# Two attention layers with film on one core: VectorE's block turns ahead of h, bulk transfers moved on SP's queue, film steps, layer change and end reordered

## The reference

```
xn = layernorm(x) * norm_scale + norm_bias
q, k, v = xn @ Wq + bq, xn @ Wk + bk, xn @ Wv + bv        # masked rows: k = -inf (or -1e6), v = 0
q = softmax(q over the head's columns);  k = softmax(k over the 128 rows)
y = q @ (k^T @ v)                                          # per head
scale, shift = split(silu(cond) @ film_W + film_b)         # one row per sequence
h = layernorm(y) * film_norm_scale + film_norm_bias
h = h * (1 + scale) + shift
x = x + silu(h) @ Wo + bo
```

## Time and profile before

| | us |
|---|---|
| runs | 969.55, 980.11, 980.13 (median 980.11) |
| profiled execution, own time | 981.22 |
| profiled execution, span | 979.4 |
| TensorE busy | 873.1 (89%) |
| VectorE, ScalarE, POOL busy | 674.4, 609.8, 555.9 |
| mean granted TensorE clock | 0.955 |
| DMA, mean over the span | 173 GB/s |

### The profile page before, as it was taken

The page is one execution under the profiler, slowest core; times in us unless marked ns, Lnnn a source line. Parts: engine busy times, 40 slices in busy tenths (PEclk is TensorE's granted clock), DMA queues, the critical chain, the costliest instruction groups (busy, mean ns, idle before and its releaser), DMA issues. The chain is left out here.

```text
span 979.4 us, 19873 instructions
## 1 busy us (share of the span) xinstructions
PE 873.1 (89%) x6581; PEld 733.7 (75%) x6581; DVE 674.4 (69%) x1349; ACT 609.8 (62%) x1445; POOL 555.9 (57%) x744
## 2 busy tenths in 40 slices
PE   5878898999889999999489899999899999999975
PEld 4657776888778887888367788887788787887753
DVE  6776675776777776777547777776777777775632
ACT  5354765665766667766455876677666776666442
POOL 2455655556556765666456665665567656665310
PEclk9898998999999999999789999999999999999987
DMA  8667666646465554554626555554565555553310
GB/s 302 217 202 223 199 197 218 211 144 200 157 205 161 162 170 141 163 166 149 209 81 221 169 174 160 182 173 170 155 192 200 182 184 176 174 188 134 123 64 32
DMA packets 115419, 169.80 MB, mean 173 GB/s; under 512 B 11742, under 2 KB 84566, under 8 KB 115318
## 3 DMA queue, kind: packets, MB, share of 16 engines
q1 hardware_dynamic: 114816, 168.08, 53.3%
q10 hardware_dynamic: 502, 0.46, 0.2%
HBM read 95.61 MB, written 72.88 MB: 172 GB/s over the span
## 5 line engine op out<-in xcount | busy, mean ns | idle before, releaser
L660 ACT ACTIVATE Z<-QT,FC,FA 128x128 f32<-128x128 f32 x240 | 99.1, 484 | 182.4 <-DMA QT<-qy_turned 182.4
L546 POOL TENSOR_TENSOR HL<-H,HH 128x512 fp32r<-128x512 f32 x60 | 77.4, 1291 | 200.4 <-ACT HH L693 191.5
L821 PE MATMUL PS<-XH,WH_k 128*128 128x256 f32 x512 | 151.3, 296 | 3.9 <-DVE WL_k L300 3.9
L821 PE MATMUL PS<-XL,WH_k 128*128 128x256 f32 x512 | 146.1, 285 | 0.0
L821 PE MATMUL PS<-XH,WL_k 128*128 128x256 f32 x512 | 146.0, 285 | 0.0
L821 PE MATMUL PS<-WH_o,HH 128*128 128x512 f32 x248 | 110.3, 445 | 13.1 <-issue 6.9
L821 PE MATMUL PS<-WH_v,XH 128*128 128x512 f32 x256 | 102.3, 400 | 14.9 <-POOL WL_v L300 12.0
L821 PE MATMUL PS<-WH_q,XH 128*128 128x512 f32 x256 | 103.4, 404 | 9.6 <-ACT Z L688 9.6
L626 ACT ACTIVATE SK<-SK,KN 128x128 f32<-128x128 f32 x256 | 98.9, 388 | 9.3 <-DVE KN L1112 9.3
L821 PE MATMUL PS<-WL_o,HH 128*128 128x512 f32 x248 | 103.2, 416 | 0.0
L821 PE MATMUL PS<-WH_o,HL 128*128 128x512 f32 x248 | 102.6, 414 | 0.0
(11 more groups left out here) (144 smaller groups left out, 2157.0 us busy)
## 6 DMA issues: line engine op xcount, KB each, us to landing
qy_turned<-QS SPq DMA_DIRECT2D x60, 512.0 KB, 3.0
QT<-qy_turned SPq DMA_DIRECT2D x240, 128.0 KB, 2.9
k_turned<-KT SPq DMA_DIRECT2D x32, 512.0 KB, 4.3
EK<-k_turned SPq DMA_DIRECT2D x128, 128.0 KB, 2.8
x_turned<-XS SPq DMA_DIRECT2D x30, 512.0 KB, 2.7
XT<-x_turned SPq DMA_DIRECT2D x120, 128.0 KB, 2.9
out_x<-X SPq DMA_DIRECT2D x32, 256.0 KB, 2.9
X<-in_x SPq DMA_DIRECT2D x9, 512.0 KB, 4.6
```

Of the source, the lines that this page charges most:

```text
L546: eng.tensor_tensor(hl_of(o), h_of(o), hh_of(o).bitcast(F32), ALU.subtract).then_inc(pool_hl, 1)
L660: z = eng.activation(Z[:, c * P:c * P + P].rearrange("p (q n) -> p q n", q=Q), src, ACT.Identity, bias=FC[l][:, c, b:b + 1], scale=FA[l][: ...
L821: mm = eng.matmul(dst, left[a](c), right[b](c), start=(c == 0 and a + b == 0), stop=(c == C - 1 and a == 1))
```

## The change

FILM_SLOTS becomes [2, 3, 7, 11, 15, 19]. On VectorE turn_x and turn_queries move in front of keys and h_mul, stat_x behind values. On SP the mask load moves from the front of an even step behind the reads; x loads and stores are done in even steps, two tiles at a time for the stores. On ScalarE h_high stands behind x_turned. Around step 32 the splits, loads and biases are reordered, and one more chunk of the value weights' low half is made on VectorE. At the end, the last tile's y gets a buffer (XN) and a PSUM bank of its own, and the order is written anew on four engines.

```diff
-        FILM_SLOTS = [1, 2, 6, 9, 12, 15]
+        FILM_SLOTS = [2, 3, 7, 11, 15, 19]
...
         def norm_at(s):
-            return stats_at(s)
+            return [4, 5, 6] if s == 1 else [s + 4] if 2 < s < NT - 4 else []
...
-        LOW_ON_DVE = [range(C), range(C), [1, 2, 3], range(2), [0, 2], [0, 2], [0, 2], [0, 2]]
+        LOW_ON_DVE = [range(C), range(C), [1, 2, 3], range(2), [0, 2], [0, 1, 2], [0, 2], [0, 2]]
...
+        def y_of(o):
+            return XN[:, 1, :] if o == t2 else YN[:, :]
+
+        def bank_ty(o):
+            return B_ATT if o == t2 else B_TY
...
 SP:
             for s in range(1, NT - 1):
                 if s == B:
                     load_second(eng, 6)
-                if s % 2 == 0 and s + 2 < NT:
-                    eng.wait_ge(dve_ka, s)
-                    load_mask(eng, s // 2 + 1)
                 if s > 1:
                     for g in x_pair_at(s):
                         write_x(g)
+                if s == B - 1:
+                    load_second_bias(2, pool_bo)
                 write_qy(s)
                 if s > 1:
                     for g in x_pair_at(s):
                         read_x(g)
+                if s == B - 1:
+                    load_second(eng, 5, [0])
                 read_qy(s)
                 if s == B - 1:
-                    load_second(eng, 5)
+                    load_second(eng, 5, [1, 2, 3])
+                    load_second_bias(0, dve_v)
                 if s % 2 == 1:
                     place_keys(s // 2)
...
+                if s % 2 == 0 and s + 2 < NT:
+                    eng.wait_ge(dve_ka, s)
+                    load_mask(eng, s // 2 + 1)
                 if s == B - 1:
-                    load_second_bias(0, dve_v)
-                    load_second_bias(2, pool_bo)
                     load_second_bias(1, dve_q)
-                if s == B + 1:
+                if s == B + 2:
                     load_second(eng, 7)
-                if s >= B + 5:
+                if s >= B + 6 and s % 2 == 0:
+                    store(s - B - 6)
                     store(s - B - 5)
-                if s == 3:
+                if s == 4:
                     eng.wait_ge(pe_film, 2)
                     wait_split(3)
-                if 3 <= s < 11:
-                    load_x(s + 3)
+                if 4 <= s < 20 and s % 2 == 0:
+                    load_x(4 + s // 2)
...
 POOL:
+                if s == B:
+                    split_low(eng, 5, low_on_pool(5))
                 if s >= 3:
                     root_y(s - 3)
-                if s == B:
-                    split_low(eng, 5, low_on_pool(5))
...
+                if s == B - 1:
+                    split_low(eng, 4, low_on_pool(4))
                 if s == B:
                     split_low(eng, 6, low_on_pool(6))
                 if 2 * FIRST <= s + 2 < NSTEP:
                     x_low(s + 2)
                 normalise_keys(s)
-                if s == B - 1:
-                    split_low(eng, 4, low_on_pool(4))
...
 ScalarE:
+                if s > 1:
+                    for n in norm_at(s):
+                        norm_x(n)
+                if s == B:
+                    split_high(5)
                 if 0 <= o:
                     film(o)
                 if s >= 3:
                     norm_y(s - 3)
-                if 0 <= o:
-                    h_high(o)
-                if s == B:
-                    split_high(6)
...
-                if s in FILM_SLOTS:
-                    conditioning_sums(FILM_SLOTS.index(s))
...
                 if s > 2 and m < NSTEP:
                     x_turned(m)
+                if 0 <= o:
+                    h_high(o)
+                if s in FILM_SLOTS:
+                    conditioning_sums(FILM_SLOTS.index(s))
+                if s == B - 1:
+                    split_high(4)
+                if s == B:
+                    split_high(6)
                 if s >= 2:
                     exp_k(i)
-                if s == B - 1:
-                    split_high(4)
...
-                if s == B - 1:
-                    split_high(5)
...
 TensorE:
-                if s == 1:
-                    conditioning(0)
...
+                if s == B:
+                    output(o)
+                    attention(j)
+                queries(i)
...
             values(t2)
+            attention(t0)
+            queries(t2)
+            turn_y(t9)
             turn_queries(t1)
-            queries(t2)
-            attention(t0)
-            turn_y(t9)
+            mix(t0)
             output(LAST_Y - 1)
-            mix(t0)
             attention(t1)
             turn_queries(t2)
+            mix(t1)
+            turn_y(t0)
+            attention(t2)
+            mix(t2)
             output(t9)
-            mix(t1)
-            attention(t2)
-            turn_y(t0)
-            mix(t2)
+            turn_y(t1)
             output(t0)
-            turn_y(t1)
+            turn_y(t2)
             output(t1)
-            turn_y(t2)
             output(t2)
...
 VectorE:
-                if s > 1:
-                    for n in stats_at(s):
-                        stat_x(n)
                 if s == B:
                     split_low(eng, 5, LOW_ON_DVE[5])
-                if s == 1:
-                    turn_queries(0)
+                if 1 < s < NT - 4:
+                    turn_x(s + 4)
                 if s > 0:
+                    turn_queries(s - 1)
                     keys(i)
                 if 0 <= o:
                     h_mul(o)
-                if 1 < s < NT - 4:
-                    turn_x(s + 4)
-                if s > 1:
-                    turn_queries(s - 1)
                 if s >= 3:
                     turn_y(s - 3)
...
                 if s > 0:
                     values(i)
-                key_sums(i)
+                if s > 1:
+                    for n in stats_at(s):
+                        stat_x(n)
                 if s == B - 1:
                     split_low(eng, 4, LOW_ON_DVE[4])
...
+                key_sums(i)
...
             mixed(t9)
+            turn_keys(t2)
             h_mul(LAST_Y - 1)
             values(t2)
             queries(t2)
+            mixed(t0)
             h_mul(t9)
             h_low(t9)
             add_x(LAST_Y - 1)
-            mixed(t0)
             mixed(t1)
-            add_x(t9)
+            mixed(t2)
             h_mul(t0)
             h_low(t0)
-            mixed(t2)
+            add_x(t9)
```

More of the change, by code:

```diff
@@ L301, in split_low, with load_second @@
                                   ALU.subtract).then_inc(low_w[w][c], 1)
-        def load_second(eng, w):
+        def load_second(eng, w, chunks=range(C)):
             src = weights[1][w % 4].rearrange("(c p) n -> p c n", p=P)
-            for c in range(C):
+            for c in chunks:
                 if w > 4:
@@ L631, in norm_y @@
                 eng.wait_ge(pool_y, o + 1)
-                eng.activation(YN[:, :], YN[:, :], ACT.Identity, bias=NBY[:, :], scale=RSY[:, :]).then_inc(act_yn, 1)
+                y = y_of(o)
+                eng.activation(y, y, ACT.Identity, bias=NBY[:, :], scale=RSY[:, :]).then_inc(act_yn, 1)
             def exp_q(j):
@@ L774, in _ @@
                     exp_k(n)
-                for n in norm_at(s):
-                    norm_x(n)
                 if s == 1:
+                    for n in norm_at(s):
+                        norm_x(n)
                     split_high(3)
-                if s == B - 1:
-                    split_high(5)
                 if s == B + 3:
@@ L783, in _ @@
             film(LAST_Y - 1)
+            h_high(LAST_Y - 1)
             norm_y(t9)
             exp_q(t0)
-            h_high(LAST_Y - 1)
+            heads(t0)
             values(t2)
-            heads(t0)
             film(t9)
             exp_q(t1)
-            heads(t1)
             h_high(t9)
             norm_y(t0)
+            heads(t1)
             exp_q(t2)
@@ L873, in turn_y @@
                 for c in range(C):
-                    mm = eng.transpose(bank(B_TY, c * P, P), YN[:, c * P:c * P + P], ident[:, :])
+                    mm = eng.transpose(bank(bank_ty(o), c * P, P), y_of(o)[:, c * P:c * P + P], ident[:, :])
                 mm.then_inc(pe_ty, 1)
@@ L1181, in mixed @@
                 eng.wait_ge(dve_yr, j + 1)
-                then(eng.bn_stats(BNY[:, :], YN[:, :]))
+                then(eng.bn_stats(BNY[:, :], y))
                 eng.wait_ge(pool_y, j)
@@ L1330, in _ @@
                     split_low(eng, 6, LOW_ON_DVE[6])
+                if s == B - 1:
+                    queries(i)
+                key_sums(i)
                 if s == 0 or s == B:
                     turn_keys(i)
-                queries(i)
-                if s != 0 and s != B:
+                for n in keys_at(s):
                     turn_keys(i)
+                    keys(n)
+                if s != B - 1:
+                    queries(i)
+                if 0 < s < NT - 2 and s != B:
+                    turn_keys(i)
```

(6 more changed lines are left out.)

25 lines of the change are left out of this document (13 added, 12 removed).

## The result

The changed kernel took **901.26 us** in the median (900.45 to 902.12), the kernel before 979.30 beside it (969.55 to 980.13): ratio 0.922 (0.917 to 0.928). The forecast was 911.

What follows compares the result with a forecast made beforehand. A circuit through three engines and SP's queue, not TensorE, was taken to pace plain steps. Terms -30, -8, -4, -11 and -16 summed to -69 on 981.2, giving 912, or 911 us against the median; range 893 to 948.

Steps and rivals of the forecast that it cites:

- Plain steps, -30: Steps 6 to 61 without film pieces or layer change: 43.4 us of excess, 30 gained by a shorter circuit, 13 left.
- sign "3.8": Plain steps: the write of q and y would come 3.8 us after film's start, against 4.93 before.
- film to film under 12.9: Plain steps: one film start to the next would take under 12.9 us, a sign of the forecast holding.
- waits on HL: TensorE waiting for h_low's result ahead of the output; appearing in plain steps, they would show the forecast wrong.
- Costed at nothing: Moving h_high on ScalarE would cost nothing; with its cover gone, 0.8 us per pair of steps, some 22 us.
- Film, -8: The four film steps in steps 6 to 31: excess falls from 20.4 us to 12, at 3.0 each.
- Rival (c): Odd film steps cost what step 9 cost, 8.4 us each: 21.6 us on the forecast, 933 us; chance 0.07.
- Start, -4: First steps: 4 us gained, with film piece 0 out of step 1 and turns some 3 us earlier; bounds -9, +3.
- Layer change, -11: Step 32: from 34.7 us to about 24, with the output's bias row loaded earlier; bounds -4, -15.
- End, -16: Behind step 61: 12 us of TensorE's idle time and 4 of the clock's part gained; bounds -8, -23.
- (a): Plain steps: the circuit stays, through exp_q and a QT landing lengthened by stores; 942 us, chance 0.20.
- (b): Every step's output: the wait moves from EK to HL, slower, +85 us over 50 steps; 1026 us, chance 0.04.

Runs made afterwards that it cites:

- e1: The changed kernel with turn_x and turn_queries put back behind h_mul on VectorE; 923.98 us.
- e2: The kernel before with only turn_x and turn_queries moved ahead of keys and h_mul on VectorE; 956.08 us against 968.24 on the same chip.
- e12: The kernel before with only h_high moved behind x_turned on ScalarE, except in step 32; 975.55 us, ratio 1.002.
- e6: The changed kernel with h_high put back ahead of x_turned on ScalarE; 911.06 us.
- e3: The changed kernel with SP's bulk as before: mask ahead of an even step's write, one store and one x load a step; 904.42 us.
- e4: The changed kernel with the last four film pieces in even steps 8, 12, 16, 20, three of their loads ending odd steps; 916.36 us.
- e7: The changed kernel with layer 1's output bias row loaded behind the keys' placing of step 31 again; 909.67 us.

## Why the prediction was right

**The bound.** That a circuit, and not TensorE, set the pace of plain steps is shown from three sides: e1 brings 19.7 us of the plain stretches back (22.7 of the time) by raising the least time from film to write from 3.85 to 4.92 us, with TensorE's work the same; e2 takes 12.2 us away on one chip by shortening it alone; e12 swaps one of TensorE's waits for another and moves nothing.

**Plain steps, -30.** Measured -31.3: 26.8 in steps 33 to 61, and in steps 6 to 31 an excess of 10.8 where 15.3 was. The 13 us that I left were 12.1 (10.8 + 1.3), but of another kind than argued. I left them because the slack was some tenths of a microsecond. In layer 1, where only that could show, 1.3 were left; of the 10.8, 9.3 are steps 6, 10, 14 and 18, two behind each load of film and x. The write came 4.8 us after film in step 40 (565.34 to 570.10) and 3.85 at the least, where I wrote 3.8: the medians of steps 33 to 58 are 4.53 in even and 5.46 in odd steps. Film now comes so early that h_mul finds VectorE still at the keys, which stand ahead of it: in step 40 tanh ended at 567.66 and h_mul started at 568.71. So my sign "3.8" was wrong, and so was "film to film under 12.9" for every other film (12.11 and 13.76), and waits on HL, which I had called a sign of being wrong, do stand in seven plain steps of layer 0 (4.3 us). The time was right all the same, since slack took it. The two sides of the circuit were worked out from one pair of steps: the 5.8 us from QT's read to film in step 39 are above the median of its kind in steps 33 to 58 (4.96; 4.21 in even steps), and the 1.77 us are the issue of the x read, which the earlier trace rows does not show. That the term came out within 1.3 us is thus partly luck.

**Costed at nothing: h_high behind x_turned.** This step failed, though not in the plain steps of layer 1. In the changed kernel it is worth 9.8 us of the time and 11.2 us of the two long stretches (7.7 + 3.5, less 1.3 in step 32) [e6]. They lie where the circuit is late: 4.9 of the 7.7 us are the four film steps, and the 3.5 the steps right behind the layer change. In steps 37 to 61 it is worth nothing, as costed. I followed what h_high does to h_low and the keys, and not what waited behind h_high on ScalarE. In the kernel before it is worth nothing [e12]. The sum did not suffer, because the terms for plain and film steps were set on the whole excess and not on this move; that is luck and no merit of the costing.

**Bulk behind the placings.** The bytes are the same; the place costs 7.1 us in layer 1 in the one trace of e3 and 2 to 3 us in the medians. That what stands ahead of a write holds it was weighed as a danger: it is seen where it is large, in landings of 8.2 us behind 1.5 MB and 8.4 behind 1 MB, and not with the two stores behind the placings (0.5 MB, issued some 7 us ahead of the next write of q and y: that landed after 2.98 us in the median of odd steps 33 to 61, and after 2.96 in steps 6 to 31, which have no stores). The Trainium skill ("DMA: Bandwidth & Descriptors", Queues, rings and completion order) lets a completion count land only after the earlier writes of its engine. The traces agree with it as far as a delayed landing behind loads of the same queue shows it (8.40 us in e4 against 2.6 to 3.0); they do not tell it from a plain sharing of the engines.

**Film, -8.** Measured -12.7: 14.4, 15.1, 14.4 and 14.4 against my 15.5 each. The term was mis-sized by its price: I took step 12's 2.9 as bare, and 1.1 of it was a wait (it had 14.40 us of busy time in the earlier trace rows, which is the very length now). Bare, a piece costs 1.8. Rival (c) fell; e4 shows that the film steps' own parity does not matter and that it does matter whether their load stands right ahead of a write. How much of the 12.7 is the new film steps and how much the circuit's slack no run tells apart.

**Start, -4**, measured -5.1. **Layer change, -11**, measured -11.0; e7 gives 7.3 of it to the one bias row. **End, -16**, measured -20.6. The idle time of TensorE fell from 20.0 to 8.9, about as taken (12); its busy time fell from 53.5 to 44.0, where I had allowed 4 of 8.6 for the clock. The whole of it came back in this trace: 1.00 against 0.84. On another chip the same order had 0.94 to 0.97 and 1.6 to 2.7 us more of busy time. That term was mis-sized, and with film it makes most of the 11.7 us between -69 and -80.7.

**Rivals.** (a) fell in its result, though half of its mechanism is there: in 12 of the 29 reads of steps 33 to 61, 11 of them in even steps, the read of QT now follows exp_q's end by 0.2 us or less, so in even steps that side is as long as the write's. But the landing stayed what it was: from the read to film 4.38 us in step 40, and in the medians of steps 33 to 58 4.23 in even and 5.19 in odd steps, against 4.21 and 4.96 before. In step 40 7.64 to exp_q's end and 4.46 from there to the next film make 12.10. (b) did not come, but its place was right: without the other edits the wait does move from EK to HL [e12], and late QT makes it 4.1 us long [e4]. Its price of +85 was wrong: in e12 the waits at the output rose by 11.6 us in steps 33 to 61 and those at EK fell by 13.4, which fits the reason given against it.

## What to carry to other kernels

When several engines and a queue form a circuit, compare its length with the busiest engine's step; if the circuit is the longer, shorten it anywhere, and don't chase the wait that the trace names, since it can move without the time moving. On a queue that carries short writes which are waited for, put bulk where the next such write is farthest away, and spread it evenly, here 1 MB a step and not 1.5. Take an experiment's gain from runs on one chip, and a stretch of steps only from a trace near the median. An order that is free in one kernel can be worth 1% in another, when the waiting instruction has others behind it: list what is queued behind each wait.

## What the runs showed of the hardware

A write of 512 KB that landed after 2.6 to 3.0 us in quiet steps landed after 8.4 us with a 1 MB load issued 1.3 us ahead of it on the same queue [e4], and after 8.2 and 5.7 us, the second write 3.7 us behind the first, with 1.5 MB of loads issued from 2.1 us ahead of the first [changed kernel, steps 8 and 9]. With a 256 KB store and a mask in front it landed after 4.4 us in the median of even steps 33 to 61, against 2.6 without [e3]. And TensorE's waits of 4.4 us at the end came with 9.5 us more of busy time: busy 53.5 us at 0.84 before, 44.0 at 1.00 after; but with one and the same order of that stretch the clock was 1.00 in one run and 0.94 in others [e6, e7].
